# Four expert numbers in one register load on TensorE, and a power in front of each following row transfer on GpSimd

## The chip, the cores and the metric
One core of one Trainium2 chip. The metric is the device time of one execution in microseconds, lower is better. The kernel is one program for the five engines (PE is TensorE, DVE VectorE, ACT ScalarE, POOL GpSimd, SP SyncE), each of which works through its own list of instructions in order and waits on semaphores that others count up.

## The reference, cut to what matters
Two transformer layers over x of 8 batches, 512 tokens, 128 features, all fp32, each layer an attention and a mixture of 8 experts behind a layer norm, with residual additions.
```python
x = x + attn0(layernorm(x), wq, wk, wv, wo)                    # 16 heads of 8, 4 key/value heads, causal
x = x + ffn0(layernorm(x), router_w, router_b, w1, w2)         # top 1 of 8 experts: silu(a) * g @ w2[e], times its probability
x = x + attn1(layernorm(x), W_q, W_dkv, W_uk, W_uv, W_o, ...)  # latent of 32, rotary positions, causal
x = x + ffn1(layernorm(x), gate_w, gate_b, w1, b1, w2, b2)     # top 2 of 8 experts: relu(x @ w1[e] + b1[e]) @ w2[e] + b2[e]
```
The expert of each token is known only on the chip. So the rows of the tokens are sorted by expert in DRAM, in tiles of 128 rows ("slots") that belong to one expert each.

## The kernel before, in words
The work is a list of steps (`all_steps`, L324). For each engine a string of letters (`ORDERS`, L217) gives the order in which it takes its steps, and `Plan.read_orders` (L450) turns it into lists; nothing is decided at run time. Attention of later batches and experts of earlier ones are interleaved in these strings.

Layer 0 has two halves of four batches with 23 slots each. Layer 1 has four groups: batches 0 to 3 (39 slots), 4 and 5 (9), 6 (8), 7 (22). That makes 46 + 78 = 124 slots.

Experts of a group go like this. DVE computes the router's choice, the place of every token's row (`rows_of`), and the expert number of every slot (`expert_of`, an int32 table in one partition, L1764). POOL sends the normalised rows with indirect DMAs to their places in `sorted_in`: one of 128 rows for each of the tiles and choices ("scatter", L1099, 96 of them). In layer 1 the second choice of a room is sent after DVE has changed the row's number ("mark", L1541), and the mark waits until the first choice's rows have landed. SP fetches sorted rows, four slots at a time ("fetch", L972 and L976), and each slot's w1 ("fetch_w1", L943), for which it reads expert numbers into registers, up to four with one call (`values_at`, L808). PE turns the rows (L1308), multiplies by w1 ("first", L1326), ACT (and DVE in layer 0) makes the hidden values (L1485, L1476, L1773), and PE multiplies by w2 of the expert ("second", L1336), found by the register `e`. In layer 0 ACT copies the output and SP stores it; POOL later gathers rows back ("combine", L1117, 32 of them) and DVE adds them to X. In layer 1 DVE adds the bias and writes one of 32 output places (L1516, tile w, `kept`), and POOL sends the 128 rows back by their numbers ("send", L1107, 78 of them). At the end SP takes the returned rows (L997), DVE weighs and adds them (L1550), SP stores.

PE takes the expert number of a slot in front of "first", one `value_load` for each slot with bounds 0 and 7 (L1318). The register is used in "second".

POOL also cuts the causal masks of the attention scores (L1088), does layer-norm powers (L1043 to L1048), and small sums. Its list has the three indirect kinds in rows; `read_orders` marks a step with `pause` when MOST_IN_A_ROW (L282) indirect steps have gone before it without another step or a pause between, and `pause()` (L1028) then puts a small instruction over constants in front, after a wait for the pause before it. The last 97 steps of POOL's list before its two additions are all indirect, the last 8 + 8 scatters and nearly all sends of layer 1 among them. 

Of the kernel before, what the change touches and what calls it, by code (L numbers as in the profile page):

```python
# [8 lines left out]
ALU = mybir.AluOpType  # L9
# [269 lines left out]
RING_OF.update({kind: "pairs" for kind in ("max", "score", "first", "rotate_k")})  # L279
XT_KINDS = ("turn", "turn_ctx")  # L280
INDIRECT = ("scatter", "combine", "send")
MOST_IN_A_ROW = 2  # L282
LOADED = 4


# [238 lines left out]
def two_layers(nc, d):  # L524
    with ExitStack() as ctx:
# [492 lines left out]
        def _(pool):  # L1018
# [9 lines left out]
            def pause():  # L1028

                if pauses[0]:  # L1030
                    pool.wait_ge(paused, pauses[0])
                pool.tensor_tensor(r_small[:, 2, 0:QT], consts[:, C_EPS:C_EPS + QT], consts[:, C_HALF:C_HALF + QT], ALU.add).then_inc(paused, 1)
                pauses[0] += 1

            for s in plan.order("pool"):
# [93 lines left out]
        def _(pe):  # L1129
# [7 lines left out]
            for s in plan.order("pe"):  # L1137
# [85 lines left out]
                elif s.kind == "m_hi":  # L1223
                    v = of("max", layer, b, s.x, (QT - 1, HALF_PAIRS - 1)).uses[0]
                    pe.wait_ge(read[v.bank], v.after)
                    room(u)
                    pe.transpose(bank[u.bank][0:HALF_HEADS * QT, 0:P], neg_max[s.x][:, :, :].rearrange("p h t -> p (h t)"),
                                 ident).then_inc(full[u.bank], 1)

                elif s.kind == "score":  # L1230
                    quad = s.x
                    if s.y == 0:
                        pe.wait_ge(stacked["m", i, quad // 2], 2 * DMA * stack_turn(s))
                    room(u)
                    for n, (x, j, off) in enumerate(UNITS[s.y]):
                        pair = 2 * quad + x
                        for k in range(2):
                            rows = slice(64 * k, 64 * k + MAXROWS)
                            ins = pe.matmul(bank[u.bank + k][:, off:off + SEQ - j * P], k_stack[i][rows, k_of(layer, pair), j * P:(j + 1) * P],  # L1239
                                            q_stack[i][rows, pair, j * P:SEQ], start=True, stop=True)  # L1240
                    ins.then_inc(full[u.bank], 1)

                elif s.kind == "values":
                    quad = s.x
                    units = [of("score", layer, b, quad, n) for n in range(len(UNITS))]
                    place = {(x, j): (expd[units[n].slot], off) for n, unit in enumerate(UNITS) for x, j, off in unit}

                    pe.wait_ge(masked, MASKS_A_QUAD * (s.n // 2) + (MASKS_A_QUAD if s.y else 1))
                    if s.y == 0 and quad == 0:
                        pe.wait_ge(*values_ready(layer, b))  # L1250
                    if s.y == 0 and quad % 2 == 0:
                        room(u)
                    for j in ((0,), (1, 2, 3))[s.y]:
                        for c in range(4):
                            p, off = place[c // 2, j]
                            col = kv_of(layer, 4 * quad + c) * VSTEP + (0 if quad % 2 else VW)
                            ins = pe.matmul(bank[u.bank][CW * c:CW * c + CW, j * P:SEQ], values[batch_of(s) % 3][:, j, col:col + CW],  # L1257
                                            p[:, c % 2, off:off + SEQ - j * P], start=(j == 0 and quad % 2 == 0), stop=(j == QT - 1 and quad % 2 == 1))
                    if s.y:
                        ins.then_inc(values_made, 1)  # L1260

                elif s.kind == "normalise":
                    v = of("values", layer, b, s.x, 1).uses[0]
                    pe.wait_ge(read[v.bank], v.after)
                    room(u)
                    for t in range(QT):
                        ins = pe.transpose(bank[u.bank][:, t * P:(t + 1) * P], ctx_raw[:, t * P:(t + 1) * P], ident)  # L1267
                    ins.then_inc(full[u.bank], 1)

                elif s.kind == "turn_ctx":  # L1270
                    v = of("normalise", layer, b, 3).uses[0]
                    pe.wait_ge(read[v.bank], v.after)
                    room(u)
                    for t in range(QT):
                        ins = pe.transpose(bank[u.bank][:, t * P:(t + 1) * P], ctx_n[:, t, :], ident)
                    ins.then_inc(full[u.bank], 1)

                elif s.kind == "project":
                    x = of("turn_ctx", layer, b)
                    pe.wait_ge(read[x.uses[0].bank], x.uses[0].after)  # L1280
                    room(u)
                    for t in range(QT):
                        ins = pe.matmul(bank[u.bank][:, t * P:(t + 1) * P], xt[x.slot][:, t * P:(t + 1) * P], (wo0, wo1)[layer][:, :])  # L1283
                    ins.then_inc(full[u.bank], 1)

                elif s.kind == "logits":
                    x = of("turn", layer, b, "half")
                    pe.wait_ge(rest_loaded, REST_LOADED)
                    pe.wait_ge(read[x.uses[0].bank], x.uses[0].after)
                    room(u)  # L1290
                    for t in range(QT):
                        ins = pe.matmul(bank[u.bank][:, t * EXPERTS:(t + 1) * EXPERTS], xt[x.slot][:, t * P:(t + 1) * P], router[layer][:, :])
                    ins.then_inc(full[u.bank], 1)

                elif s.kind == "places":
                    n = EXPERTS * GT
                    each = chosen[:, :, :].rearrange("p e t -> p (e t)")
                    pe.wait_ge(chosen_made, s.n + 1)
                    room(u)
                    pe.matmul(bank[u.bank][:, 0:n], tri_bf, each)  # L1300
                    pe.matmul(bank[u.bank][:, n:2 * n], ones_bf[:, :], each).then_inc(full[u.bank], 1)

                elif s.kind == "turn_rows":
                    pe.wait_ge(fetched[s.slot], rows_landed(of("fetch", layer, b, s.x)))
                    room(u)
                    for t in range(rows_of_group(layer, b, s.x)):
                        first = t * widths[layer]
                        ins = pe.transpose(bank[u.bank][:, t * P:(t + 1) * P], rows_in[s.slot][:, first:first + DIM], ident)  # L1308
                    ins.then_inc(full[u.bank], 1)

                elif s.kind == "first":
                    r = of("turn_rows", layer, b, s.x // 4)
                    w = of("fetch_w1", layer, b, s.x)
                    if s.x == 0:
                        pe.wait_ge(w2_loaded[layer], W2_LOADED)
                        pe.wait_ge(experts_known, ALL_GROUPS.index((layer, b)) + 1)
                    j = first_slot(layer, b) + s.x
                    reg[layer, b, s.x] = pe.value_load(expert_of[half_of(layer, b)][0:1, j:j + 1], min_val=0, max_val=EXPERTS - 1)  # L1318
                    if s.x % 4 == 0:
                        pe.wait_ge(read[r.uses[0].bank], r.uses[0].after)  # L1320
                    pe.wait_ge(w1_fetched[layer][w.slot], DMA * (w.turn + 1))
                    rows = rows_t[r.slot][:, (s.x % 4) * P:(s.x % 4 + 1) * P]
                    for n, v in enumerate(s.uses):
                        room(v)
                        for c in range(FCH):
                            ins = pe.matmul(bank[v.bank][:, c * P:(c + 1) * P], w1_now[layer][w.slot][:, n * FFN + c * P:n * FFN + (c + 1) * P], rows)  # L1326
                        ins.then_inc(full[v.bank], 1)

                elif s.kind == "second":
                    h = of("first", layer, b, s.x)  # L1330
                    hidden = h.uses[-1]
                    pe.wait_ge(read[hidden.bank], hidden.after)
                    room(u)
                    e = reg.pop((layer, b, s.x))
                    for k in range(FCH):
                        ins = pe.matmul(bank[u.bank][:, 0:P], hidden_t[h.slot][:, k * P:(k + 1) * P],  # L1336
                                        w2[layer][:, bass.ds(e, 1), k * DIM:(k + 1) * DIM].rearrange("p a n -> p (a n)"),
                                        start=(k == 0), stop=(k == FCH - 1))
                    ins.then_inc(full[u.bank], 1)
# [523 lines left out]
```

## Time and profile before
| what | us |
|---|---|
| median of 3 timed runs | 961.73 |
| lowest and highest | 957.59, 963.76 |
| span of the one profiled execution, first to last instruction | 1045.8 |
| PE busy in it | 891.1 |
| POOL busy in it | 533.1 |

The profiled execution is a run of its own, with every instruction recorded. What it took beyond its span isn't listed, so its own time is the span and a little more; it is already 84 us above the timed median. An idle engine's row names what it waited for: a line of another engine, "issue" (nothing that the profile shows), or "remote", a release by nothing that the profile knows in this program.

### The profile page before, as it was taken

How to read it: one execution, taken by the hardware profiler on the slowest of the kernel's cores; microseconds unless marked ns; L12 is line 12 of the kernel's file. 1: busy time of each engine (PE TensorE's matmuls, PEld its weight loads, DVE VectorE, ACT ScalarE, POOL GpSimd, SP SyncE). 2: the span in 40 equal slices, each digit the busy share in tenths (PEclk: the TensorE clock that was granted, in tenths of full speed). 3: DMA queues.
4: the chain of work that ended last, by engine and by line, in shares of the span. 5: the costliest groups of instructions: out<-in, count | busy, mean ns of one | idle time of the engine just before them, and what ended most of it. 6: DMA issues, size and time to landing. Idle time of an engine off the chain costs nothing.

```text
span 1045.8 us, 24961 instructions
## 1 busy us (share of the span) xinstructions
PE 891.1 (85%) x8968; PEld 594.2 (57%) x8968; DVE 671.7 (64%) x1379; ACT 608.6 (58%) x1173; POOL 533.1 (51%) x809
## 2 busy tenths in 40 slices
PE   4699999879998999689999899979887776579991
PEld 2344544436995445349984445534435766578891
DVE  1889898757546988875578897898872261011117
ACT  3178897825444876745336967775684533245551
POOL 3144444573003886773037865678767443645443
PEclk9999999879999999889999998998999898789996
DMA  5635632362755162527935173345223354547767
GB/s 146 140 85 150 166 73 70 85 178 81 219 170 157 54 167 76 118 89 231 269 131 122 49 168 101 94 107 160 52 56 92 100 160 138 149 139 227 207 196 228
DMA packets 137314, 141.17 MB, mean 135 GB/s; under 512 B 35564, under 2 KB 113452, under 8 KB 137100
## 3 DMA queue, kind: packets, MB, share of 16 engines
q1 hardware_dynamic: 130604, 126.04, 44.3%
q0 software_dynamic: 6592, 13.55, 4.1%
q8 instruction: 76, 1.25, 0.5%
q14 instruction: 42, 0.34, 0.1%
HBM read 98.73 MB, written 44.36 MB: 137 GB/s over the span
## 4 chain that ended last, share of the span: by engine, by line
PE 33%; DVE 6%; another core or an unknown queue 5%; issue 4%; ACT 3%; DMA 2%; SPq 1%; POOL 1%; DVEq 0%; ACTq 0%; POOLq 0%
PE psum L1326 9%; PE psum L1336 8%; PE psum L1257 4%; PE psum L1213 2%; DVE neg_max L1519 2%; PE psum L1239 2%; ACT scratch L1448 1%; PE psum L1219 1%; PE psum L1308 1%; PE psum L1283 1%; PE psum L1175 1%; DMA w<-sorted_out,rows_of 1%; PE psum L1267 1%; DVE X L1550 1%
## 5 line engine op out<-in xcount | busy, mean ns | idle before, releaser
L1519 DVE TENSOR_REDUCE neg_max<-psum 128x2 f32<-128x768 f32 (+3 forms) x352 | 380.4, 1120 | 69.0 <-PE psum L1219 48.7
L1448 ACT ACTIVATE scratch<-psum 128x1024 f32<-128x1024 f32 x320 | 316.2, 1024 | 97.2 <-PE psum L1239 81.8
L1088 POOL TENSOR_SCALAR_AFFINE_SELECT scratch<-scratch 128x512 f32<-128x512 f32 x256 | 158.3, 639 | 155.3 <-ACT scratch L1448 154.6
L1326 PE MATMUL psum<-rows_t,w_now 128*128 128x128 f32 x1360 | 177.6, 284 | 5.4 <-issue 3.7
L1326 PEld LDWEIGHTS psum<-rows_t,w_now 128*128 128x128 f32 x1360 | 165.5, 198 | 14.0 <-issue 11.5
L1257 PE MATMUL psum<-scratch,values 128*32 128x512 f32 (+3 forms) x2048 | 170.9, 455 | 1.3 <-POOL scratch L1088 0.3
L1336 PE MATMUL psum<-w,hidden_t 128*128 x992 | 138.3, 288 | 35.3 <-DVE w L1516 14.7
L1213 PE MATMUL psum<-k_stack,q_stack 52*128 52x128 bf16 (+3 forms) x1024 | 135.2, 323 | 26.4 <-ACT scratch L1448 10.5
L1485 ACT ACTIVATE hidden_t<-psum,w_now 128x128 f32<-128x128 f32 x312 | 88.5, 372 | 113.6 <-remote 46.8
L1336 PEld LDWEIGHTS psum<-w,hidden_t 128*128 128x128 f32 x992 | 125.6, 201 | 42.3 <-issue 42.1
L1239 PE MATMUL psum<-q_stack,k_stack 55*128 55x512 bf16 (+3 forms) x1024 | 123.9, 315 | 14.8 <-ACT scratch L1448 6.5
L1516 DVE TENSOR_TENSOR w<-psum,w_now 128x128 f32<-128x128 f32 x78 | 22.7, 291 | 164.3 <-PE psum L1336 101.5
L1099 POOL DMA_INDIRECT sorted_in<-xn_half,rows_of x96 | 94.1, 980 | 47.6 <-DVE xn_half L1541 25.1
L1107 POOL DMA_INDIRECT returned<-w,goes_to x78 | 76.8, 984 | 70.1 <-DVE w L1516 38.4
L1213 PEld LDWEIGHTS psum<-k_stack,q_stack 52*128 52x128 bf16 x1024 | 43.7, 98 | 104.4 <-issue 41.1
L1219 PE MATMUL psum<-masks_bf 64*128 64x64 bf16 (+2 forms) x1408 | 94.1, 212 | 2.5 <-issue 2.5
L1257 PEld LDWEIGHTS psum<-scratch,values 128*32 128x32 f32 x2048 | 55.8, 112 | 64.6 <-issue 43.8
L1219 PEld LDWEIGHTS psum<-masks_bf 64*128 64x128 bf16 x1408 | 71.4, 101 | 35.2 <-issue 10.3
L1239 PEld LDWEIGHTS psum<-q_stack,k_stack 55*128 55x128 bf16 x1024 | 37.0, 96 | 74.7 <-issue 32.9
L1773 DVE SCALAR_TENSOR_TENSOR hidden_t<-w,psum 128x512 f32<-128x512 f32 x46 | 31.6, 687 | 58.6 <-PE psum L1336 33.4
L1070 POOL TENSOR_TENSOR rot<-rot 128x512 f32<-128x512 f32 x16 | 20.3, 1271 | 49.5 <-DVE rot L1516 49.0
L1078 POOL TENSOR_TENSOR max_parts<-max_rest,max_parts 32x128 bf16<-32x128 f32 x32 | 13.5, 422 | 58.8 <-ACT max_parts L1344 58.6
(141 smaller groups left out, 1024.2 us busy)
## 6 DMA issues: line engine op xcount, KB each, us to landing
w_now<-in_w SPq DMA_DIRECT2D x78, 322.0 KB
w_now<-in_w SPq DMA_DIRECT2D x46, 512.0 KB
q_stack<-q_parts SPq DMA_DIRECT2D x64, 192.0 KB
q_parts<-q_parts SPq DMA_DIRECT2D x16, 384.0 KB, 2.9
k_stack<-k_parts SPq DMA_DIRECT2D x32, 192.0 KB
q_parts<-q_parts SPq DMA_DIRECT2D x16, 256.0 KB, 3.0
w<-in_w SPq DMA_DIRECT2D x16, 256.0 KB, 4.6
scratch<-returned SPq DMA_DIRECT2D x16, 256.0 KB, 3.6
```

The lines of the kernel that those rows point to most:

```text
L1088: pool.affine_select(out=diag, in_=diag, compare_op=ALU.is_ge, fill=0.0, base=0, pattern=[[0, 4], [1, P]], channel_multiplier=-1).then_inc ...
L1099: pool.indirect_dma_start(sorted_in[s.layer][half_of(s.layer, g)][:, :], bass.IndirectOffsetOnAxis(ap=row_of(s.layer, g, t, k), axis=0), x ...
L1107: pool.indirect_dma_start(returned[h][:, :], bass.IndirectOffsetOnAxis(ap=goes_to[h][:, j:j + 1], axis=0), kept[slot], None).then_inc(sent ...
L1213: pe.matmul(out[:, j * width:(j + 1) * width], q_stack[i][rows, pair, t * P:(t + 1) * P], k_stack[i][rows, k_of(layer, pair), 0:width], st ...
L1219: ins = pe.matmul(blocks, ident_of[half, :], mask[half, :].unsqueeze(1).to_broadcast([P // 2, n, P // 2]), start=False, stop=(first > widt ...
L1239: ins = pe.matmul(bank[u.bank + k][:, off:off + SEQ - j * P], k_stack[i][rows, k_of(layer, pair), j * P:(j + 1) * P], q_stack[i][rows, pai ...
L1257: ins = pe.matmul(bank[u.bank][CW * c:CW * c + CW, j * P:SEQ], values[batch_of(s) % 3][:, j, col:col + CW], p[:, c % 2, off:off + SEQ - j ...
L1326: ins = pe.matmul(bank[v.bank][:, c * P:(c + 1) * P], w1_now[layer][w.slot][:, n * FFN + c * P:n * FFN + (c + 1) * P], rows)
L1336: ins = pe.matmul(bank[u.bank][:, 0:P], hidden_t[h.slot][:, k * P:(k + 1) * P], w2[layer][:, bass.ds(e, 1), k * DIM:(k + 1) * DIM].rearran ...
L1448: act.activation(expd[s.slot], psum[:, u.bank:u.bank + 2, :], ACT.Exp, scale=SCALE).then_inc(read[u.bank], 1)
L1485: ins = act.activation(hidden_t[s.slot][:, c * P:(c + 1) * P], bank[u.bank][:, c * P:(c + 1) * P], ACT.Relu, bias=w[:, FFN + c:FFN + c + 1])
L1519: return dve.tensor_reduce(out=out, in_=in_, axis=AX, op=op, negate=negate)
```

## The change
PE's expert numbers come four at a time: at every fourth slot one call loads the numbers of up to four slots into registers, without the run-time check of bounds. MOST_IN_A_ROW becomes 1, so each indirect step that directly follows another gets a pause. The instruction of a pause, an addition over 4 columns of constants in 128 partitions, becomes a power over 2 columns.
```diff
-MOST_IN_A_ROW = 2
+MOST_IN_A_ROW = 1
 LOADED = 4
...
-                pool.tensor_tensor(r_small[:, 2, 0:QT], consts[:, C_EPS:C_EPS + QT], consts[:, C_HALF:C_HALF + QT], ALU.add).then_inc(paused, 1)
+                pool.tensor_tensor(r_small[:, 2, 0:2], consts[:, C_EPS:C_EPS + 2], consts[:, C_HALF:C_HALF + 2], ALU.pow).then_inc(paused, 1)
...
-                    j = first_slot(layer, b) + s.x
-                    reg[layer, b, s.x] = pe.value_load(expert_of[half_of(layer, b)][0:1, j:j + 1], min_val=0, max_val=EXPERTS - 1)
+                    if s.x % LOADED == 0:
+                        n, j = min(LOADED, SLOTS[layer][b] - s.x), first_slot(layer, b) + s.x
+                        found = nc.values_load_multi_w_load_instructions(
+                            expert_of[half_of(layer, b)][0:1, j:j + n], engines=[mybir.EngineType.PE], min_val=0, max_val=EXPERTS - 1,
+                            skip_runtime_bounds_check_because="the table is made on the chip of counts that cannot leave these bounds")
+                        for k, e in enumerate(found[1]):
+                            reg[layer, b, s.x + k] = e
```

## Rows read from the trace of the kernel before

**Rows 1.** The page: span, busy times, and the chain that ended last by line.
```profile
span 1045.8 us, 24961 instructions
...
PE 891.1 (85%) x8968; PEld 594.2 (57%) x8968; DVE 671.7 (64%) x1379; ACT 608.6 (58%) x1173; POOL 533.1 (51%) x809
...
PE psum L1326 9%; PE psum L1336 8%; PE psum L1257 4%; PE psum L1213 2%; DVE neg_max L1519 2%; PE psum L1239 2%; ACT scratch L1448 1%; PE psum L1219 1%; PE psum L1308 1%; PE psum L1283 1%; PE psum L1175 1%; DMA w<-sorted_out,rows_of 1%; PE psum L1267 1%; DVE X L1550 1%
```

**Rows 2.** Windows: length, busy PE, PEld, DVE, ACT, POOL (instructions), PE clock, DMA.
```profile
205.00:235.00 30.00, 21.06 (x209) 10.22 (x209) 19.06 (x27) 9.90 (x14) 21.78 (x29) 0.83 0.57 160
...
250.00:320.00 70.00, 69.89 (x624) 65.66 (x624) 36.19 (x59) 31.93 (x67) 6.66 (x13) 1.00 0.61 192
...
893.00:919.00 26.00, 10.87 (x67) 9.92 (x65) 0.91 (x4) 3.66 (x13) 19.50 (x27) 0.71 0.39 113
919.00:1030.00 111.00, 98.86 (x783) 93.60 (x783) 20.50 (x80) 58.49 (x200) 53.37 (x73) 0.95 0.67 196
```

**Rows 3.** Waits from 795 to 919 us: us in total, times, longest.
```profile
DVE w L1516 <- remote: 44.4, 7, 16.7
ACT hidden_t L1485 <- remote: 44.0, 6, 11.8
...
POOL sorted_in L1099 <- DVE xn_half L1541: 25.1, 2, 13.9
```

**Rows 4.** Timeline, two freezes: start, length, instruction, [idle before and its end].
```profile
227.13 0.65 PE L1159 MATMUL psum<-xn_t,wkv 128*32 128x128 f32 x4 [0.51 <-issue]
...
232.89 0.60 ACT L1344 ACTIVATE ctx_raw<-psum 128x512 f32<-128x512 f32 x1 [14.54 <-remote]
...
918.67 0.29 DVE L1516 TENSOR_TENSOR w<-psum,w_now 128x128 f32<-128x128 f32 x1 [16.72 <-remote]
```

**Rows 5.** Timeline of ACT and POOL at 451 us, between two pairs of scatters.
```profile
451.25 1.02 ACT L1448 ACTIVATE scratch<-psum 128x1024 f32<-128x1024 f32 x1 [0.49 <-PE psum L1239]
...
451.59 0.64 POOL L1088 TENSOR_SCALAR_AFFINE_SELECT scratch<-scratch 128x512 f32<-128x512 f32 x1
```

**Rows 6.** PE's loads, ns min/median/max; then idle time of PE before L1326.
```profile
L1318 PEldq TENSOR_LOAD <-expert_of x124: 295/302/910, 251.3 to 1020.3; - x124
L1318 PEldq FUSED_REGOPS  x124: 146/151/165, 251.8 to 1020.6; - x124
L1318 PEldq SEQ_ASSERT  x124: 18/18/28, 252.1 to 1020.8; - x124
...
  issue: 15.2, 41
```

**Rows 7.** SP's loads of up to four expert numbers, 880 us to the end.
```profile
L810 SPq TENSOR_LOAD <-expert_of x14: 284/604/1007, 887.9 to 1014.3; - x14
```

**Rows 8.** Timeline of PE's weight loads in the last stretch.
```profile
966.57 1.08 PEld L1326 LDWEIGHTS psum<-rows_t,w_now 128*128 128x128 f32 x9 [0.20 <-issue]
```

**Rows 9.** Waits from 920 to 1025 us, PE's weight loads of the first product.
```profile
PEld psum L1326 <- issue: 3.0, 12, 0.5
```

**Rows 10.** Groups of POOL's instructions: busy us, mean ns, idle before.
```profile
L1088 POOL TENSOR_SCALAR_AFFINE_SELECT scratch<-scratch 128x512 f32<-128x512 f32 x256 | 158.3, 639 | 155.3 <-ACT scratch L1448 154.6
...
L1046 POOL TENSOR_TENSOR ln_small<-ln_small,consts 128x4 f32<-128x4 f32 x40 | 41.2, 1031 | 3.1
...
L1032 POOL TENSOR_TENSOR route_small<-consts 128x4 f32<-128x4 f32 x62 | 13.0, 209 | 1.6
```

**Rows 11.** Timeline of POOL: scatters with (before 895.73, 898.38) and without a pause.
```profile
895.73 1.00 POOL L1099 DMA_INDIRECT sorted_in<-xn_half,rows_of  x1 [0.16 <-issue]
897.03 0.96 POOL L1099 DMA_INDIRECT sorted_in<-xn_half,rows_of  x1 [0.30 <-issue]
...
898.38 1.00 POOL L1107 DMA_INDIRECT returned<-w,goes_to  x1 [0.16 <-issue]
```

**Rows 12.** The chain that ended last, its end: start, us, what.
```profile
1026.17 2.43 DMA returned<-w,goes_to
...
1032.92 3.43 DMA scratch<-returned
```

## The prediction

> **What bounds the kernel now.** I read the page first: PE is busy 85% of the span, DVE 64%, and the chain that ended last is mostly PE lines, the two expert products in front [rows 1]. Then the windows by stage. Three kinds of stretch are to be seen [rows 2]. In 250 to 320 us (experts of layer 0, first half) PE is busy 69.89 of 70 us: PE is the bound. In 919 to 1030 us (experts of layer 1) it is busy 98.86 of 111. But in 893 to 919 us PE works 10.87 of 26 us while POOL is busy 19.50: there POOL issues 18 row transfers one behind the other. The third view are the waits: in 795 to 919 us DVE waited 44.4 us and ACT 44.0 us for "remote", that is for no instruction the profile knows [rows 3]. The timeline shows when. POOL issued 11 transfers from 217.1 to 231.3 us, and ACT, whose input PE had finished, stood still until 232.89 (14.54 us), while PE sat idle 0.51 us even before small matmuls that wait for nothing; the last freeze holds DVE 16.72 us, to 918.67 [rows 4]. Nine runs of three and more transfers end so, with the others going on 0.6 to 2.1 us after the last one. Where 0.64 us of another POOL instruction lies between pairs of transfers, ACT goes on beside them, as at 451.25 [rows 5]. So the profiled execution suffers from transfers in a row, and 0.21 us of pause after every second one doesn't cure it.
>
> Is that so in the timed executions? The span is 1045.8 us [rows 1] and the median 961.73, 84 us less; launch and end would even add to the latter. How much do freezes cost in the trace? At the pace of 919 to 1030 us (783 PE matmuls in 111 us, 0.142 us each) the 67 matmuls of 893 to 919 need 9.5 us, so 16.5 us are lost; the same for the three other stretches of layer 1 gives about 12 us more, and PE's idle time in 205 to 235 is another 9 [rows 2]. With two small ones that is some 45 us, less than the 84 by which the timed runs are shorter. So I take it that the timed runs have none of the freezes; they belong to the profiled execution. During a freeze even a matmul that waits for nothing comes late [rows 4], which fits records that can't be written.
> The Trainium skill has a rule for that: "NOTIFIC — the notification-queue block", section 7.1, says that the block's internal pipeline always pushes back on whoever makes records rather than lose one. By that rule the freezes exist only where instructions are traced; if instead semaphores themselves were held up, the timed runs would share them (a rival below).
>
> **The change, part 1: TensorE's loads.** Each of 124 slots now has a load (median 302 ns), a register operation (151) and an assertion (18) in PE's sequencer [rows 6]: 0.47 us, 0.59 from the first start to the last end. SP already loads up to four numbers with one TENSOR_LOAD, without the other two, median 604 ns over a stretch with freezes in it, 284 at least [rows 7]. After: 33 loads (6+6 in layer 0; 10+3+2+6 in layer 1, where 22 slots make 6), 91 fewer, and no operations behind them. How much of it was in the open? The sequencer runs ahead of the array while matmuls queue, so most loads are hidden: PE sat idle before the first product 15.2 us in 41 gaps in all [rows 6], but a typical one in the end stretch is the 0.20 us at 966.57 [rows 8], and there all such gaps sum to 3.0 us of weight loading in 12 [rows 9], besides gaps under the view's threshold. Measured from weight load to weight load, less 0.11 us of normal spacing, I count 0.9 us where the load ended last in layer 0, about 3.7 in 785 to 905 and 4.4 after it. A load remains in one of four slots. So at most 9, likely 6 us of PE time go: 1 in layer 0, 5 in layer 1; none is the other end.
> The four-register load could cost more than I take: the Trainium skill, "Runtime: NRT & Kernel Launch", section "Instruction fetch mechanics", gives some 200 ns for each register even in bulk, an estimated 0.8 us for four. SP's 284 ns minimum disagrees, and with it 33 loads of 0.3 us are the smaller price.
>
> **Part 2: POOL's pauses.** They stood in front of every third transfer of a row (62); now in front of each that follows another. Counted along the order string that makes 156, 94 more: 21 for the scatters of layer 0, 14 for its gathers, 43 for the scatters of layer 1 and 78 for its sends (before: 6, 2, 14 and 40). No trace row shows a power over two columns. Over four it takes 1031 ns, the addition over four 209 [rows 10]. Bounds: 0.21 us (power as cheap as the add) and 1.03 (no gain from fewer columns). The difference, 0.82 us for four columns, looks like work by the column, so half of it: 0.21 + 0.41 = 0.62 us. It is nearest to the row of the wide power, halved.
> From start to start, two transfers without a pause take 1.30 us (0.30 of it idle), with a pause 1.35 (1.00 + 0.21 + gaps of 0.02 and 0.16) [rows 11]. With the power: 0.98 + 0.02 + 0.62 + 0.16 = 1.78 us, each. So a row of n transfers grows from 1.33 n to 1.78 n, +0.45 each; by the bounds +0.04 to +0.86. The new wait on the last pause is for POOL's own, long finished instruction; behind it queue masks, layer-norm powers and transfers.
>
> Where does it show in a run without freezes?
> - 208 to 231 us: 16 scatters, +5.7 us. Masks queue behind; in the trace the first mask behind them was asked for only at 237.7 because of the freeze. Taking ACT's 11.5 lost us out (its input was ready about 221.4) and giving back 2.6 us of PE work done meanwhile, PE would want the masked scores near 235.2 and gets them at 237.0 + 0.65: +2.4 (0 to 5.7).
> - Masks and gathers among attention, 320 to 795 us: POOL idles 154.6 us waiting for ACT before masks [rows 10], which hides most of it: +1.5 (0 to 4).
> - 795 to 892 us: 41 transfers in front of the last marks, +18 us of POOL work, against some 43 us in which POOL waited, 25.1 for DVE's marks alone [rows 3]; part of that waiting is freeze. The mark of one room waits for its scatters to land and stands in DVE's order before later outputs. +1.5 (0 to 6).
> - From 892.4 us: then 4 scatters and 63 sends are left: 67 x 1.78 = 119 us. PE's side: 48 outputs from 918.7 to 1025.1 us, 2.22 each, 51 of them 113 us, 1 more to the send. Now POOL needs 67 x 1.33 = 89 and catches up: its sends come 0.76 us behind the output at the end. After, POOL ends last. +5 by the trace's durations; as the timed runs are shorter also outside freezes (961.7 against about 1001) PE's pace may be 4% faster there, which makes +9. I take +6. PE's 5 us of gain in layer 1 is then worth nothing: the output ring has 32 places, so PE runs ahead and the last send sets the end. The bounds: -5 at 0.21 us a pause (POOL stays hidden and PE's gain counts), 67 x 2.19 = 147, +33, at 1.03.
> The rest behind the last send (landing 2.43, take-back 3.43, the additions) stays [rows 12].
>
> **Sum** for the timed run: 2.4 + 1.5 + 1.5 + 6 - 1 (loads in layer 0) = +10.4 us on 961.7: **972 us**. For the profiled execution, against its own 1045.8: the same +10, and the freezes gone as 0.8 us lie between transfers: -45, about 1011 us. I expect the profile to shrink and the time to grow. A measurement of this kernel tells about 1% from nothing.
>
> **Rivals.**
> 1. Freezes in the timed runs too. For it: ACT waited for a semaphore, not for a record, and the freezes sit where transfers do. Against: the 84 us. If so, 45 us go, or half when milder, POOL's cost and PE's gain about cancel: 917 to 940 us. Chance 0.22.
> 2. POOL hidden throughout (power nearer 0.3 us, or the last sends catch up): only the loads' gain, -6, and +2 in layer 0: 957 us. Decides at the pause for which 67 intervals fit in 109 us: 1.63 each, a power of 0.47 us. Chance 0.2.
> 3. The power costs 1.03 us: the last stretch alone +33, with the others +45: about 1007 us, slower. Chance 0.06.
> 4. Nothing moves: loads hidden by queued matmuls, POOL covered: 962. Chance 0.08.
> My forecast has 0.44, its own range 964 to 988.
>
> **Chances.** Faster by over 1% (below 952): rival 1 and a little of 2: 0.25. Within 1%: most of 2, 4 and a third of mine: 0.35. Slower: the rest of mine and 3: 0.4. Range 938 to 988, leaving out the deeper half of rival 1 and rival 3.
>
> **What would show it.** Right: the pause group at x156 with about 620 ns; "remote" waits gone; 33 PE loads near 300 ns with nothing behind; POOL's sends falling ever further behind DVE's outputs after 895 us, PE done 5 us or more before the last send; span near 1011. Wrong: sends 0.76 us behind at the end (rival 2), or a median well under 950 (rival 1).

## The result: slower by 6.8%, and the profile after

| | before | after |
|---|---|---|
| median | 961.31 us (957.59 to 963.76, 4 runs) | 1025.76 us (1023.77 to 1028.33, 4 runs) |
| ratio | | 1.068, 95% interval 1.065 to 1.070 |
| profiled execution: time, span | span 1045.8 (the one shown ahead) | 1024.31, span 1022.5 |

972 was forecast, 938 to 988 as the range. The profiled execution of after stands with its median. That of before did not: it took 84 us more than the timed runs, and much of what the forecast got wrong was read from it.

The page of after, to be read against [rows 1]: span, busy times and the chain that ended last.
```profile
span 1022.5 us, 24716 instructions
...
PE 873.0 (85%) x8968; PEld 580.9 (57%) x8968; DVE 672.9 (66%) x1379; ACT 609.9 (60%) x1173; POOL 642.8 (63%) x903
...
PE 47%; POOL 23%; DVE 14%; issue 7%; ACT 4%; DMA 4%; SPq 1%; POOLq 0%; DVEq 0%; ACTq 0%
```
POOL has 94 instructions more and 110 us more of work, and is 23% of the chain.

The groups of POOL of after (busy us, mean ns of one, idle time before), to [rows 10]; the last line is the source view of PE's loads (ns min/median/max), to [rows 6].
```profile
L1032 POOL TENSOR_TENSOR route_small<-consts 128x2 f32<-128x2 f32 x156 | 114.2, 732 | 4.9
L1046 POOL TENSOR_TENSOR ln_small<-ln_small,consts 128x4 f32<-128x4 f32 x40 | 41.2, 1029 | 3.1
```
```profile
L1319 PEldq TENSOR_LOAD <-expert_of x33: 313/335/1134, 249.8 to 972.4; - x33
```
156 pauses and 33 loads, as counted. A pause is 0.73 us; 0.62 was forecast.

The timeline of POOL at the end of after (start, length, instruction, idle before), to [rows 11].
```profile
999.49 1.03 POOL L1107 DMA_INDIRECT returned<-w,goes_to  x1 [0.19 <-issue]
1000.55 0.73 POOL L1032 TENSOR_TENSOR route_small<-consts 128x2 f32<-128x2 f32 x1
1001.47 1.03 POOL L1107 DMA_INDIRECT returned<-w,goes_to  x1 [0.19 <-issue]
1002.54 0.72 POOL L1032 TENSOR_TENSOR route_small<-consts 128x2 f32<-128x2 f32 x1
1003.46 1.03 POOL L1107 DMA_INDIRECT returned<-w,goes_to  x1 [0.20 <-issue]
```
And the last output of the second product on DVE, same kernel:
```profile
978.49 0.29 DVE L1521 TENSOR_TENSOR w<-psum,w_now 128x128 f32<-128x128 f32 x1 [0.24 <-PE psum L1341]
```
From start to start a transfer takes 1.99 us (1.78 forecast), without any wait in between, and the last send starts 24.7 us after the last output has ended. The windows say the same: length, busy PE, PEld, DVE, ACT, POOL, granted clock, DMA share and GB/s.
```profile
871.00:978.00 107.00, 99.83 (x840) 97.37 (x841) 17.15 (x66) 62.25 (x212) 94.86 (x109) 0.97 0.77 231
978.00:1004.00 26.00, 0.45 (x5) 0.26 (x3) 8.23 (x30) 0.00 (x0) 23.07 (x26) 0.59 0.10 33
```
For 26 us POOL works nearly alone: PE is busy for 0.45 us and ACT not at all, and DVE's 8.23 us are additions over rows that have come back.

The waits for "remote" of [rows 3] are gone, as forecast. But against what? The first experiment answers that.

### The profile page after: what moved, and what is told of

Same layout as the page of the kernel before. It is cut to its first block, busy times and chain, and to the rows that moved or that the text cites. A ratio compares the mean times of both kernels' runs of the same rounds, so it can differ in the third digit from the quotient of the medians.

```text
span 1022.5 us, 24716 instructions
## 1 busy us (share of the span) xinstructions
PE 873.0 (85%) x8968; PEld 580.9 (57%) x8968; DVE 672.9 (66%) x1379; ACT 609.9 (60%) x1173; POOL 642.8 (63%) x903
## 4 chain that ended last, share of the span: by engine, by line
PE 47%; POOL 23%; DVE 14%; issue 7%; ACT 4%; DMA 4%; SPq 1%; POOLq 0%; DVEq 0%; ACTq 0%
PE psum L1331 13%; PE psum L1341 9%; POOL sorted_in L1099 8%; PE psum L1257 7%; DVE neg_max L1524 7%; POOL route_small L1032 6%; PE psum L1239 4%; PE psum L1213 4%; POOL scratch L1088 3%; POOL returned L1107 3%; ACT scratch L1453 2%; PE psum L1219 1%; DMA w<-sorted_out,rows_of 1%; PE psum L1308 1%; DVE ln_small L1579 1%
## 5 line engine op out<-in xcount | busy, mean ns | idle before, releaser
L1088 POOL TENSOR_SCALAR_AFFINE_SELECT scratch<-scratch 128x512 f32<-128x512 f32 x256 | 158.2, 640 | 126.1 <-ACT scratch L1453 125.1
L1257 PE MATMUL psum<-scratch,values 128*32 128x512 f32 (+3 forms) x2048 | 174.6, 462 | 13.8 <-POOL scratch L1088 13.2
L1331 PE MATMUL psum<-rows_t,w_now 128*128 128x128 f32 x1360 | 172.2, 280 | 6.4 <-DMA w_now<-in_w 4.2
L1331 PEld LDWEIGHTS psum<-rows_t,w_now 128*128 128x128 f32 x1360 | 162.6, 196 | 10.8 <-issue 8.8
L1341 PE MATMUL psum<-w,hidden_t 128*128 x992 | 132.1, 280 | 6.9 <-ACT hidden_t L1490 1.7
L1341 PEld LDWEIGHTS psum<-w,hidden_t 128*128 128x128 f32 x992 | 120.6, 194 | 11.9 <-issue 11.7
L1032 POOL TENSOR_TENSOR route_small<-consts 128x2 f32<-128x2 f32 x156 | 114.2, 732 | 4.9
L1099 POOL DMA_INDIRECT sorted_in<-xn_half,rows_of x96 | 98.1, 1022 | 19.9 <-issue 17.2
L1107 POOL DMA_INDIRECT returned<-w,goes_to x78 | 80.9, 1037 | 15.1 <-issue 13.4
L1778 DVE SCALAR_TENSOR_TENSOR hidden_t<-w,psum 128x512 f32<-128x512 f32 x46 | 31.6, 688 | 58.4 <-PE psum L1341 33.0
```

The source lines that it names most:

```text
L1032: pool.tensor_tensor(r_small[:, 2, 0:2], consts[:, C_EPS:C_EPS + 2], consts[:, C_HALF:C_HALF + 2], ALU.pow).then_inc(paused, 1)
L1088: pool.affine_select(out=diag, in_=diag, compare_op=ALU.is_ge, fill=0.0, base=0, pattern=[[0, 4], [1, P]], channel_multiplier=-1).then_inc ...
L1099: pool.indirect_dma_start(sorted_in[s.layer][half_of(s.layer, g)][:, :], bass.IndirectOffsetOnAxis(ap=row_of(s.layer, g, t, k), axis=0), x ...
L1107: pool.indirect_dma_start(returned[h][:, :], bass.IndirectOffsetOnAxis(ap=goes_to[h][:, j:j + 1], axis=0), kept[slot], None).then_inc(sent ...
```

## The experiments

They came in five sets; the kernels of a set share a chip and the runs of the kernel before beside them. An interval in square brackets is the 95% interval of the ratio to the kernel before, and outputs are those of layer 1's 78 slots, counted from 0. Before measured 961.49 us (29 runs, 956.65 to 965.82) in the first set, 1047.53 (17 runs, 1041.31 to 1057.23) in the second, 962.36, 963.22 and 961.27 in the other three. A time is compared within its set alone.

### The kernel before again, and each half of the change alone (before: 961.49)

> The kernel before, unchanged, for a second trace. Theory A (freezes belong to some executions, the recorded one by chance or by its way of recording, and the others have none): time 958 to 964 us; if this trace is of an ordinary execution, its span lies 2 us under its time, waits for 'remote' over 3 us are absent, and the outputs of layer 1's last 51 slots need some 109 to 114 us. Rival B (freezes are part of every execution, and 1045.8 us is another cost): 'remote' waits of some 40 us each on DVE and ACT again in a run of 961 us.

The kernel before, unchanged: 962.61 us (8 runs), its profiled execution 963.93. The page of that execution:
```profile
span 962.1 us, 24961 instructions
...
PE 864.1 (90%) x8968; PEld 575.3 (60%) x8968; DVE 670.8 (70%) x1379; ACT 608.9 (63%) x1173; POOL 533.1 (55%) x809
...
PE 34%; DVE 9%; issue 3%; DMA 3%; ACT 1%; SPq 1%; POOL 0%; DVEq 0%; ACTq 0%; POOLq 0%
```
Its waits hold no "remote" at all, and POOL is 0% of the chain. (The chains are no like measure of the two kernels: this one could be followed back over half of the span only, as its shares show, that of after over all of it. In the third execution of the whole change it reaches half of the span too, and there POOL has 14%.) So the same kernel has freezes in one profiled execution and none in another. This profile, not the one shown ahead, is the one to compare after with.

> Part 1 alone: the four-at-a-time register loads, pauses as before. Theory P (the whole loss is POOL's pauses; the loads give what was reckoned): 4 to 8 us faster than before, 953 to 957 us, 33 TENSOR_LOADs of some 0.3 us and no idle gap before the first product from the sequencer in three of four slots. Rival L (the four-register load costs more than it saves, at the heads of groups of four): slower than before by 1 us or more.

Only the loads:
```diff
-                    reg[layer, b, s.x] = pe.value_load(...)
+                    if s.x % LOADED == 0:
+                        ...
```
960.51 us (12 runs), ratio 0.9986 [0.9965, 1.0007]; repeated in the third set 959.86 beside 962.36, 0.9983 [0.995, 1.0015]. The medians differ by 1.0 and 2.5 us, 4 to 8 were expected, and neither can be told from nothing. PE's weight loads of the first product, groups of the kernel before again and of this one:
```profile
L1326 PEld LDWEIGHTS psum<-rows_t,w_now 128*128 128x128 f32 x1360 | 160.7, 193 | 14.5 <-issue 11.7 <-ACT rows_t L1344 1.2 <-DMA w_now<-in_w 0.3
```
```profile
L1331 PEld LDWEIGHTS psum<-rows_t,w_now 128*128 128x128 f32 x1360 | 160.7, 193 | 10.4 <-issue 7.5 <-ACT rows_t L1349 1.2 <-DVE w L1521 1.2
```
Idle time that "issue" ended fell by 4.2 us; how much of that reached the end, the times can't tell.

> Part 2 alone: a power over two columns in front of each following transfer, PE's loads as before. Theory P: as slow as the whole change or up to 3 us slower, 1024 to 1029 us, since POOL sets the pace of the last stretch and PE's gain is worth nothing there; start to start of two transfers 1.99 us. Rival L: clearly faster than the whole change, under 1015 us.

```diff
-MOST_IN_A_ROW = 2
+MOST_IN_A_ROW = 1
...
-                pool.tensor_tensor(r_small[:, 2, 0:QT], consts[:, C_EPS:C_EPS + QT], consts[:, C_HALF:C_HALF + QT], ALU.add).then_inc(paused, 1)
+                pool.tensor_tensor(r_small[:, 2, 0:2], consts[:, C_EPS:C_EPS + 2], consts[:, C_HALF:C_HALF + 2], ALU.pow).then_inc(paused, 1)
```
1021.53 us, ratio 1.061 [1.0575, 1.0645]: the pauses alone cost 60 us. The whole change cost 64.5 in the runs of the result and 61.7 and 61.8 in later sets, so the pauses are the loss; 1024 to 1029 had been expected.

> The addition over four columns (0.21 us) in front of each following transfer, loads as before: as many pauses (156) as the change, each shorter. Theory P (length of the pause counts): start to start 1.42 us at most, POOL keeps up with PE in the last stretch, 961 to 967 us. Rival N (the number of pauses and their waits counts, not their length): over 990 us.

MOST_IN_A_ROW = 1 with the old addition: 963.91 us, ratio 1.0021 [1.0000, 1.0042]. 156 short pauses in place of 62 cost 2.4 us, at most 4 by the interval; it is their length that costs.

### Beside a kernel before that takes 1047.53 us

In this set each of 17 executions of the kernel before took over 1041 us, and the chip was the one of the first set, 40 minutes later.

> No pause instruction at all; start to start 1.30 us everywhere. Theory P (pauses only cost): 0 to 2 us faster than before. Rival S (long rows of transfers hold up semaphores or records of the others, and the pauses prevent it): waits for 'remote' in the trace and times tens of us above before, in some or all executions.

MOST_IN_A_ROW = 1000, no pause at all: 1048.19 us, ratio 1.0007 [0.9976, 1.0037]. Its profiled execution took 1046.15. Its waits over the whole span (us in total, times, longest):
```profile
DVE w L1516 <- remote: 48.1, 6, 13.2
ACT hidden_t L1485 <- remote: 41.5, 6, 17.2
ACT ctx_raw L1344 <- remote: 17.7, 3, 13.8
DVE neg_max L1519 <- remote: 17.4, 5, 9.1
```
The kernel before was not profiled in this set. But all its timed executions take what this kernel takes, and what the profile with freezes ahead of the prediction takes, so the freezes are in the timed executions here, and the additions of 0.21 us after every second transfer do nothing against them.

> The power over two columns, but only where the addition was before (62 pauses, in front of every third of a row). Start to start 1.30 and 1.99 in turn, 1.65 in the mean. Theory P: in the last stretch 67 x 1.65 = 110 us, just PE's pace, so nothing there, and about half of the 34 us in front of it: 972 to 982 us. If the number of pauses mattered beyond their length, less.

The power over two columns where the kernel before has its addition, after every second transfer: 989.23 us (4 runs, 982.05 to 998.5), ratio 0.9464 [0.9402, 0.9526]. What is left of the waits:
```profile
ACT ctx_raw L1344 <- remote: 4.5, 1, 4.5
ACT scratch L1448 <- remote: 4.3, 2, 2.3
DVE neg_max L1519 <- remote: 3.8, 3, 1.8
```

> The power over one column instead of two, in front of every following transfer. From 0.73 us for two and 1.03 for four columns: 0.15 a column, 0.58 us, start to start 1.84. Theory P: 67 x 1.84 = 123 us in the last stretch against PE's 110, 12 to 13 us there, and three quarters of the 34 us in front of it: 995 to 1003 us. Rival H (a power costs the same for one column, a fixed price): 1020 us.

A power over one column ahead of every transfer that follows another: 1000.54 us, ratio 0.9543 [0.9491, 0.9596], no "remote" wait. The timeline gives 0.57 us for a power. From start to start it is 1.90 us in these rows, whose first transfer is a long one (1.11), and 1.83 in 45 of the last 50.
```profile
961.13 0.57 POOL L1032 TENSOR_TENSOR route_small<-consts 128x1 f32<-128x1 f32 x1
961.89 1.11 POOL L1107 DMA_INDIRECT returned<-w,goes_to  x1 [0.20 <-issue]
963.03 0.57 POOL L1032 TENSOR_TENSOR route_small<-consts 128x1 f32<-128x1 f32 x1
963.79 1.04 POOL L1107 DMA_INDIRECT returned<-w,goes_to  x1 [0.19 <-issue]
```

> A pause in front of every following transfer, the 0.73 us power only in front of layer 1's 78 sends, the 0.21 us addition elsewhere; PE's loads as before. Theory P (POOL's list is the bound of the end): nothing changes up to the first send; from the output of slot 26 on 4 scatters at 1.40 and 63 sends at 1.99 us need 131 us, the last send goes some 20 us behind the last output, and up to 9 us more come from the 15 sends in front of the last marks: 981 to 992 us. Rival Q (the sends are covered by the 32 output places, and the loss comes from scatters and masks): under 970 us.

Two columns ahead of the sends, the addition elsewhere: 1031.7 us, ratio 0.981 [0.975, 0.988]. The 981 to 992 expected were for a kernel before near 961 us. The freezes went for the most part where the long pauses are, and stayed elsewhere:
```profile
ACT ctx_raw L1347 <- remote: 25.5, 3, 14.3
DVE neg_max L1522 <- remote: 16.9, 6, 6.3
DVE w L1519 <- remote: 9.4, 2, 6.7
```
DVE's wait at the outputs, 48.1 us without pauses, is 9.4.

### The price by place, where there are no freezes (before: 962.36, then 963.22)

One place at a time gets the long pause, all others the addition:
```diff
-MOST_IN_A_ROW = 2
+MOST_IN_A_ROW = 1
...
+                if long:
+                    pool.tensor_tensor(r_small[:, 2, 0:2], consts[:, C_EPS:C_EPS + 2], consts[:, C_HALF:C_HALF + 2], ALU.pow).then_inc(paused, 1)
+                else:
...
-                    pause()
+                    pause(s.kind == "send")
```


> The power over two columns ahead of the 77 sends of layer 1 that follow one another, the addition in all other gaps. If the kernel before stands near 961 us this prices the send term alone: 67 transfers from the last mark on at 1.99 us are 133 us against the 109 that TensorE needs from there, so 24 us over the kernel before, 983 to 988 us; the rival, that the marks' stretch ahead of it carries a part of it, gives 988 to 1000 us. If it stands near 1047 us: 1023 to 1034 us as in the first run of this kernel.

> The power over two columns ahead of layer 0's scatters alone, the addition in all other gaps. Theory 1 (every scatter of layer 0 is waited for by the group that reads the sorted rows): 14 powers longer by 0.52 us in each of the two sets of 16 scatters, some 7 us each, the first in full on the path and the second in most of it, as the marks of the whole change show (10 us late when the first gathered rows are read, 16 us late at the second group): 12 to 17 us over the kernel before if that stands near 961 us. Theory 2 (the delay is taken up again by slack before layer 1): 0 to 6 us.

> The power over two columns ahead of layer 1's scatters alone. In the whole change TensorE's experts of layer 1 start 9 us later against the start of layer 1's scatters than in the kernel before, and the 26 slots after that take 10 us more, of which the powers before the sends alone gave 3. Theory 1 (these are the scatters' own): 9 to 17 us over the kernel before where that stands near 961 us. Theory 2 (they come of the sum of all pauses, GpSimd having fallen behind its plan in layer 0 already): 0 to 6 us.

> The power over two columns ahead of the 16 gathering transfers that combine layer 0 alone. Between the second group and the start of layer 1's scatters the whole change lost 1 to 5 us. Theory: 1 to 5 us over the kernel before where that stands near 961 us. Rival (VectorE, which adds what is gathered, takes each row later and the whole tail of layer 0 is late by 16 times 0.52 us): 7 to 9 us.

| long pause ahead of | median | over before | ratio, 95% interval |
|---|---|---|---|
| the sends | 987.60 | 25.2 | 1.0278 [1.0197, 1.036] |
| scatters of layer 0 | 975.24 | 12.0 | 1.0135 [1.0085, 1.0186] |
| scatters of layer 1 | 976.67 | 13.5 | 1.0130 [1.0077, 1.0183] |
| gathers of layer 0 | 970.17 | 7.0 | 1.0064 [1.0032, 1.0097] |
| sum | | 57.7 | |
| the whole change, run beside the first of them | 1024.04 | 61.7 | 1.0625 [1.0555, 1.0696] |

> The whole change, unchanged, beside the kernel before on the same chip at the same time. What the kernel before costs depends on when it is run: 961 us with no wait on something remote in one set of runs, 1047 us with such waits in every one of 17 executions in the next set. Theory 1 (the long pauses remove the freezes and cost some 62 us of their own): this kernel takes 1020 to 1030 us in either condition, so the ratio is 1.06 to 1.07 if the kernel before stands near 961 us, and 0.97 to 0.985 if it stands near 1047 us. Theory 2 (what slows the second condition slows everything, and the pauses only lengthen GpSimd's work): the ratio is near 1.06 in both, so 1105 us or more beside 1047 us.

The places add up to the whole within their intervals, and these are wide. Each of the four kernels also has the 94 further additions, which alone cost 2.4 us; counted once and not four times, the sum is 50.5, so up to 11 us may be interplay. In one stretch the traces show some: from output 0 to output 26 the whole change takes 10.2 to 11.6 us more than the kernel before again (four executions), while the long pauses of the sends alone make 3.4 and those of layer 1's scatters alone 3.5. The sends (24 expected), layer 0's scatters and layer 1's came out as the first theory had them in size, though layer 0's have 12 long pauses in the first 16 and 9 in the second, 21 as counted in the prediction, and not 14 each. The gathers' median is the rival's price, 7 to 9, and not 1 to 5; its interval, 3.1 to 9.3 us, leaves both. Their trace has 7.7 us more from the second scatters of layer 0 to the first of layer 1 (266.5 for 258.8); that DVE's additions pass it on, as the rival has it, is not shown.

Where it arises, from the profiles. In the sends, DVE's last output and POOL's last send of that kernel; 22.6 us lie between the starts, and 1.0 in the kernel before again (940.98 and 942.03).
```profile
942.03 0.29 DVE L1519 TENSOR_TENSOR w<-psum,w_now 128x128 f32<-128x128 f32 x1 [0.24 <-PE psum L1339]
```
```profile
964.66 1.03 POOL L1110 DMA_INDIRECT returned<-w,goes_to  x1 [0.20 <-issue]
```
In the scatters of layer 0 (expected: 12 to 17) PE waits for a mask that stands behind 16 of them in POOL's order. PE's waits from 205 to 250 us, of the kernel with that pause and, second, of the kernel before again:
```profile
PEld psum L1260 <- POOL scratch L1091: 6.1, 1, 6.1
PE psum L1260 <- POOL scratch L1091: 6.0, 1, 6.0
```
```profile
PEld psum L1257 <- POOL scratch L1088: 0.2, 1, 0.2
```
From the first scatter to the first read of the sorted rows it takes 38.9 us (204.9 to 243.8), and 31.6 (204.4 to 236.0) in the gathers' kernel, which has the addition there: 7.3 us. In layer 1's scatters it is masks again, behind the transfers that lie among the attention. The wait of PE's weight loads from 680 to 773 us (1.1 us in all in the kernel before again), and the windows of that stretch (from the first scatter of layer 1 to the first output of its experts), first that kernel, then the kernel before again:
```profile
PEld psum L1260 <- POOL scratch L1091: 9.3, 9, 2.0
```
```profile
680.50:773.20 92.70, 78.81 (x911) 39.89 (x915) 76.14 (x152) 63.75 (x91) 79.45 (x111) 0.93 0.31 84
```
```profile
678.40:761.40 83.00, 74.64 (x911) 39.26 (x915) 74.74 (x153) 63.15 (x91) 65.71 (x92) 0.98 0.35 94
```
9.7 us more for the same 911 records of PE. POOL's 13.7 us more of work are not hidden by its waits for ACT, though it still has them (3.9 us here, 3.6 in the kernel before again). 4.2 us of the 9.7 are PE being busy longer, with a granted clock of 0.93 and not 0.98: a wait costs its length and some matmuls at 1.2 GHz behind it.

### From what length on a pause costs

> The loads of four, and the shortest long pause, a power over one column (0.57 us), where the kernel before has its addition: after every second transfer. Per pair of transfers that is 0.36 us more than before, 0.18 us per transfer. Theory (the cost goes with the mean interval of the transfers, the power over one column at every transfer having cost 39 us for an interval longer by about 0.5 us): some 10 to 15 us over the kernel before of the free condition, 968 to 978 us, in either condition if every second gap is enough against the freezes. Rival (a mean interval below that of the run with two columns at every second transfer doesn't hold the freezes off): 968 to 978 us if the kernel before stands near 961 us, but over 1000 us if it stands near 1047 us.

> Two columns where the kernel before has its addition, after every second transfer: 989.2 us in the condition with freezes, where small waits on something remote, 13 us in all, were left. In the condition without: the sends' interval is 1.38 us in one half and 1.99 us in the other, 1.69 us in the mean, below the 2.15 us that one output takes TensorE, so GpSimd keeps up in the sends and that term is nothing; the scatters cost half of what they cost in the whole change. Theory: 961 us plus 5 to 18 us, 966 to 979 us. Rival (what is short in the mean is short everywhere, as with one column): 960 to 965 us.

One column at every second transfer, with the loads: 961.40 us beside 962.36, ratio 0.9994 [0.9961, 1.0028], and in the fifth set 964.46 beside 961.27, 1.0032 [1.0, 1.0063]: nothing that is clear of noise, and at most 6 us. I had expected 968 to 978. Two columns at every second transfer: 970.36 beside 963.22, 1.0073 [1.0042, 1.0104]. Its sends take 1.34 and 1.90 us in turn:
```profile
937.28 1.03 POOL L1107 DMA_INDIRECT returned<-w,goes_to  x1 [0.19 <-issue]
938.62 0.96 POOL L1107 DMA_INDIRECT returned<-w,goes_to  x1 [0.30 <-issue]
939.59 0.73 POOL L1032 TENSOR_TENSOR route_small<-consts 128x2 f32<-128x2 f32 x1
940.52 1.03 POOL L1107 DMA_INDIRECT returned<-w,goes_to  x1 [0.19 <-issue]
```
A send starts how long after its output has ended? In the kernel before again 24.9 us at output 21, where the marks of layer 1 have held POOL up, and 0.8 at output 44 and never over 1.6 from there on; with two columns at every second 29.2 and then 1.3 at the last; with two columns at every one 34.6 and then 21 to 26 from output 28 to the last. All three are behind at output 21. What differs is whether they catch up.

The last set was a try for the other condition.

> The whole change again. Theory 1 (long pauses remove the freezes): 1020 to 1030 us whether the kernel before stands near 962 us or near 1047 us. Theory 2 (the slow condition adds to everything): 1105 us or more beside 1047 us.

It didn't come up. The whole change took 1023.07 us beside 961.27, 1.061 [1.051, 1.071].

## Why the prediction was wrong

**Freezes: the conclusion holds, the reason falls.** "So I take it that the timed runs have none of the freezes" is right for these runs of the kernel before. But "they belong to the profiled execution" is not: the profiled execution with a span of 962.1 us has none, and in the second set all 17 executions of the kernel before took 1041 us and more, beside a profile full of freezes of the kernel without pauses. They come with a condition that holds for a whole set of runs, on the same chip in one set and not in another; why the one profiled execution ahead of the prediction had them beside timed runs of 961 us is not shown. The Trainium skill's "NOTIFIC — the notification-queue block", section 7.1, on a pipeline that pushes back on whoever makes records, was my ground. Recorded executions without any freeze, as the one with a span of 962.1 us, show that recording isn't enough for one. Whether it is needed, no run shows. The "45 us, less than the 84" was no evidence for more gaps elsewhere either: between the freezing execution and the kernel before again, 12 us are gone when the first sorted rows are read, 61.9 at output 26 of layer 1 and 83.7 at the end; 2.8 of them lie ahead of the first transfer, where executions without freezes differ by up to 4.4, and the others behind it. I priced only the big stops.

**Part 1, the loads.** Count and kind were right, and SP's rows were the better guide to the price: four numbers in 335 ns. By the Trainium skill's "Runtime: NRT & Kernel Launch", section "Instruction fetch mechanics", they would have taken an estimated 800 (that section has the runtime's own register loads in view, and these read a table on the chip); the trace disagrees. The gain, "likely 6 us", was 1 to 2.5 by the medians. I read gaps from an execution with freezes: 15.2 us of "issue" in [rows 6] are 12.1 by the same view in the undisturbed one, and 8.3 of these stay.

**Part 2, the price of a pause.** The step that took half of the difference between the addition and the wide power, 0.62 us, failed by 0.11. A power has a fixed part: 0.57, 0.73 and 1.03 us for one, two and four columns are 0.42 and 0.15 for each column. The transfer behind it takes 1.03 us, not 0.98, and the gap 0.20, not 0.16. So 1.99 us from start to start, not 1.78, +0.21 each.

**Part 2, the last stretch.** The step was sound: 67 transfers from the last mark on against what PE needs for 51 outputs. After, the last mark is at 870.8 us, and 67 x 1.99 = 133 us later is 1003.8; the last send starts at 1003.46. Two sizes were off: the interval, 67 x 0.21 = 14 us, and PE's side, which takes 109.6 us from output 26 to the last (110.4 in the kernel before again) and not 113. 6 was forecast, 21.6 to 23.9 measured: the 22.6 us (the sends' kernel) and 25.0 us (after) between the last starts, less the 1.0 of the kernel before again. My bounds, -5 to +33, held it; I took the wrong place in them. The same sum fits the one-column run, whose sends come every 1.84 us in the mean of the last 50 and whose outputs take 108.9 us: 67 x 1.84 - 108.9 = 14.4, and the last send starts 14.4 us after the last output does.

**Part 2, "masks and gathers" and the rest: the step that failed worst.** It said that 154.6 us of POOL's waiting for ACT hide most of the pauses among the attention and 1.5 us are left, with 2.4 at the first scatters and 1.5 at 795 to 892 us. Measured from stage to stage, after against the kernel before again: 7.7 us from the first scatter to the first read of sorted rows; 16.1 from there, over the masks, gathers and attention, to output 0 of layer 1 (9.2 of it from layer 1's first scatter on); 11.6 from there to output 26. Together 35.3 us, and 5.4 forecast; three other executions with all the long pauses give 34 to 37. The two traces lie 60.4 us apart, 50 more than the forecast's 10.4: 30 of these are here and 16 in the last stretch. The rest is 3 us ahead of the first pause, within what executions without freezes differ by there, and the 1 us that the loads didn't give back. POOL's wait was summed over masks from 53 to 794 us, but a transfer delays the mask that stands right behind it, and slack at another time doesn't help: POOL of after still waits 125.1 us for ACT, and PE, which waited 0.3 us for masks, waits 13.2. The groups of after and, second, of the kernel before again:
```profile
L1257 PE MATMUL psum<-scratch,values 128*32 128x512 f32 (+3 forms) x2048 | 174.6, 462 | 13.8 <-POOL scratch L1088 13.2
```
```profile
L1257 PE MATMUL psum<-scratch,values 128*32 128x512 f32 (+3 forms) x2048 | 171.9, 456 | 1.3 <-POOL scratch L1088 0.3
```
At the first scatters I worked the size out from an execution with a 14.54 us stop in just that place and subtracted what the stop had hidden. Without it PE of after wants the masks at 232.8 us and gets them at 240.34 (the row stands at the end of this text); it had been 235.2 and 237.65 in the forecast. So the powers show in full.

**Rivals.** Rival 1 (the timed runs share the freezes) is wrong for these runs and right for the second set. There too its price, 917 to 940 us, was not met by any version: no execution went below 982 us in that set, and the whole change wasn't run in it. Rival 2 named the point of decision, 1.63 us an interval: at 1.62 in the mean (two columns at every second) POOL just catches up, at 1.84 it doesn't. It says nothing of the costs ahead of the sends, and I had none of size there in any case. Rival 3's 1007 us was nearest, for the wrong reason.

**The signs.** 156 pauses, no "remote", 33 loads with nothing behind them, PE done 25 us ahead of the last send: as named. The pause's length was not, 732 ns and not 620. The sends don't fall ever further behind, they fall behind once and stay there. The span, 1011 forecast, was 1022.5; the profile shrank and the time grew, as said.

**What stays open.** What brings the condition with freezes (one set of five had it; the last three sets ran on three other chips), and what the whole change takes in it, which was never run under it. The one-column version had no freeze there and stood at 1000.5 us; as the whole change has none either, an estimate from its time without freezes is 1020 to 1030 beside 1047. Nor was the version with powers that costs nothing clear of noise, one column at every second transfer, run under it. Where there are no freezes, no version here beats the kernel before by more than noise; where there are, two columns at every second transfer did best of the four that were run, 989 us.

## What to carry to other kernels

Before a profile is costed, set its time beside the timed runs: 84 us apart means that it shows another condition, and every wait, slack and gap in it has to be read again from an execution at the median. Slack of an in-order engine counts only where it stands right behind the added work, not in the sum over a stage. And an engine that falls behind once has to win it back: compare its interval with its partner's times the number of turns left, and not its busy share.

## What the runs showed of the hardware

- A power on POOL over 128 partitions takes 0.57, 0.73 and 1.03 us for one, two and four columns; an addition over four 0.21.
- Row transfers in a row can freeze the other engines, for up to 17.2 us at a time. The same program on the same chip took 1041 us or more in all of 17 executions at one time and under 966 in all of 29 forty minutes earlier, 86 us between the medians. Pauses of 0.21 us after every second transfer take as long as none at all (1047.53 and 1048.19 us), 0.57 us ahead of each following transfer leave no freeze, 0.73 us after every second leave 13 us of waits.
- A wait of PE costs more than its length. After, PE stands still for 7.56 us ahead of the masks, and the eight products that follow take 1.93 us; at the same place of the kernel before again 1.06.
```profile
240.34 1.93 PE L1257 MATMUL psum<-scratch,values 128*32 128x512 f32 x8 [7.56 <-POOL scratch L1088]
```
```profile
231.82 1.06 PE L1257 MATMUL psum<-scratch,values 128*32 128x512 f32 x8
```
The windows give a granted clock of 0.66 from 240 to 248 us of after and of 1.00 from 232 to 240 of the other, so most of the first window runs at 1.2 GHz and all of the second at 2.4:
```profile
240.00:248.00 8.00, 7.66 (x72) 2.47 (x74) 1.22 (x2) 3.15 (x4) 4.38 (x8) 0.66 0.25 76
```
```profile
232.00:240.00 8.00, 7.98 (x108) 3.42 (x101) 5.43 (x7) 4.26 (x7) 5.12 (x9) 1.00 0.32 92
```
